# Order of selections, logits, one-hot transposes and scatters in a mixture-of-experts stage

## The reference

```python
grouped = x.reshape(B, S // t, t, D)                 # t = 16 tokens in a group
cont_logits = jnp.einsum('bgtd,des->bgtes', grouped, controller) + tie
cont_perm = (cont_logits == jnp.max(cont_logits, axis=-3, keepdims=True))
intermediate = jnp.einsum('bgtd,desf->bgtesf', grouped, f1)
inner = jax.nn.relu(jnp.einsum('bgtesf,bgtes->bgesf', intermediate, cont_perm))
inter2 = jnp.einsum('bgesf,esfd->bgesd', inner, f2)
result = jnp.einsum('bgesd,bgtes->bgtd', inter2, cont_perm)
```

## Time and profile before

| | us |
|---|---|
| median of 3 runs (lowest, highest) | 752.02 (750.18, 753.73) |
| the profiled execution's own time | 753.89 |
| its span, first to last instruction | 752.0 |
| PE busy | 711.2 (95%) |
| DVE busy | 595.7 (79%) |
| ACT busy | 544.2 (72%) |
| chain that ended last, share of PE | 86% |
| chain that ended last, share of DVE and of DMA | 6% and 2% |

### The profile page before, as it was taken

How to read it: one execution, slowest core, us unless ns; L and a number is a source line. 1 busy time by engine, 2 the same in 40 slices (tenths; PEclk the granted TensorE clock), 3 DMA queues, 4 the chain that set the end, 5 groups by cost and what they waited for, 6 DMA issues and landing times.

```text
span 752.0 us, 22953 instructions
## 1 busy us (share of the span) xinstructions
PE 711.2 (95%) x7420; PEld 575.8 (77%) x7420; DVE 595.7 (79%) x2418; ACT 544.2 (72%) x1606; POOL 181.2 (24%) x375
## 2 busy tenths in 40 slices
PE   8899999999999999999999999989879979878888
PEld 7788888888888888888888888866656656655666
DVE  6698898898988988989889888986656756656566
ACT  4788989898889898988899889874445344344243
POOL 2130321302303213023032130646705506400000
PEclk9999999999999999999999999998999999999999
DMA  6776787677867877778678767746099798798943
GB/s 179 185 184 143 185 196 163 166 187 166 193 147 177 194 164 167 185 168 193 150 174 194 166 144 157 158 87 218 3 394 300 261 388 276 265 383 271 342 164 104
DMA packets 110742, 149.24 MB, mean 198 GB/s; under 512 B 14784, under 2 KB 75712, under 8 KB 110432
## 3 DMA queue, kind: packets, MB, share of 16 engines
q1 hardware_dynamic: 107904, 146.26, 72.0%
q10 hardware_dynamic: 2592, 1.71, 1.0%
q0 software_dynamic: 192, 0.52, 0.2%
HBM read 39.39 MB, written 33.55 MB: 97 GB/s over the span
## 4 chain that ended last, share of the span: by engine, by line
PE 86%; DVE 6%; issue 3%; DMA 2%; ACT 2%; SPq 1%; POOL 0%; DVEq 0%; POOLq 0%
PE bank L672 15%; PE bank L624 15%; PE bank L659 8%; PE bank L685 8%; PE bank L696 8%; PE bank L646 7%; PE bank L819 5%; PE bank L861 3%; DVE stage L1503 3%; PE bank L904 3%; DMA stage<-scratch 2%; PE bank L717 2%; PE bank L877 2%; PE bank L617 2%; PE bank L704 2%
## 5 line engine op out<-in xcount | busy, mean ns | idle before, releaser
L1026 ACT ACTIVATE Ps<-Ps,nmax 128x256 f32<-128x256 f32 x512 | 254.6, 501 | 19.8 <-DVE nmax L1246 19.8
L1246 DVE CUSTOM_DVE_ANT_0 Ps<-bank,masks 128x256 f32<-128x256 f32 x512 | 193.0, 421 | 28.6 <-issue 28.4
L672 PE MATMUL bank<-ident,Ps 128*128 128x128 f32 x1024 | 134.8, 274 | 2.5 <-ACT Ps L1026 1.8
L672 PEld LDWEIGHTS bank<-ident,Ps 128*128 128x128 f32 x1024 | 114.8, 141 | 11.9 <-issue 3.3
L624 PE MATMUL bank<-hT,WT 128*128 128x256 f32 x512 | 121.1, 380 | 0.3 <-ACT hT L983 0.3
L624 PEld LDWEIGHTS bank<-hT,WT 128*128 128x128 f32 x512 | 92.4, 190 | 10.7 <-ACT Vs L999 0.7
L549 POOL TENSOR_SCALAR h<-X,mv,roots 128x256 f32<-128x256 f32 x64 | 79.6, 1255 | 78.7 <-PE bank L819 76.5
L1026 ACT ACTIVATION_READ_ACCUMULATOR Ps<-Ps,nmax 128x1 f32 x512 | 97.4, 190 | 0.0
L659 PE MATMUL bank<-stack 128*128 128x256 f32 x512 | 91.5, 311 | 0.6 <-DMA stack<-parts 0.6
L1257 DVE COPY PTs<-bank 128x512 f32<-128x512 f32 x128 | 86.7, 677 | 0.2
L659 PEld LDWEIGHTS bank<-stack 128*128 128x128 f32 x512 | 71.7, 189 | 17.3 <-issue 13.1
(11 more groups left out here) (107 smaller groups left out, 1052.9 us busy)
## 6 DMA issues: line engine op xcount, KB each, us to landing
stack<-parts SPq DMA_DIRECT2D x506, 128.0 KB, 2.5
scratch<-stage SPq DMA_DIRECT2D x48, 512.0 KB, 4.3
stage<-scratch SPq DMA_DIRECT2D x96, 256.0 KB, 4.4
X<-in_x SPq DMA_DIRECT2D x32, 256.0 KB, 2.9
out<-X SPq DMA_DIRECT2D x32, 256.0 KB, 3.7
rbc<-turned SPq DMA_DIRECT2D x126, 64.0 KB, 2.1
f1s<-in_L_ffn_f SPq DMA_DIRECT2D x1, 2048.0 KB, 8.5
f2s<-in_L_ffn_f SPq DMA_DIRECT2D x1, 2048.0 KB, 14.2
```

The lines of the kernel that those rows point to most:

```text
L672: last = nc.tensor.transpose(PTb[h % 2][:, k * N + t * P:k * N + t * P + P], Ps[:, pr % 2, t, h % 2, k * P:k * P + P], ident[:, :])
L1026: last = nc.scalar.activation(Ps[:, pr % 2, t, h, :], Ps[:, pr % 2, t, h, :], ACT.Exp, bias=nmax[:, pr % 2, t, h:h + 1], scale=-1.0, accum ...
L1246: last = nc.vector.tensor_tensor_reduce(out=Ps[:, pr % 2, t, h, :], in0=s_bank(n)[:, h * N:h * N + N], in1=masks[:, t, :], scale=1.0, scal ...
```

## The change

It does four things.

1. In each unit the one-hot transpose leaves its place between the first and second selection and goes between the third and fourth, with bank 3 in place of bank 2. It then waits until DVE has finished the pair that was in bank 3 (`fin_done`; in unit 1 of chunk 0 `res_done`). Unit 0 of chunk 0 keeps its place. ACT's save of it moves in the same way.
2. The logits no longer wait for the saved one-hot (`perm_saved`), but for DVE's comparison (`perm_done`).
3. A unit's first scatter moves from behind the third selection to behind the first; its second stays behind the fourth and waits in addition for `perm_saved`. On DVE the maximum now stands in front of the third save, and the first `finish` between the first and second save.
4. In the last chunk the units scatter pairs 0 and 1, then 2, then 3 and 4, and the expert stage pairs 5, 6, 7 in rounds 1, 2, 3; its three-way rotation of banks starts two rounds later, at round 4.

```diff
+        def scatters(c, u):
+            return ((), (0, 1), (2, 3), (4, 5))[u] if c < CHUNKS - 1 else ((), (0, 1), (2,), (3, 4))[u]
+        def late(c, w):
+            return {0: 6, 1: 7}.get(w) if c < CHUNKS - 1 else {1: 5, 2: 6, 3: 7}.get(w)
+        TWO_PAIRS = 4
...
             def logits(n, into=bank[2]):
-                if n > 0:
+                if n > AHEAD:
+                    pe.wait_ge(perm_done, n)
+                elif n > 0:
                     pe.wait_ge(perm_saved, n)
...
                 select(n, 0)
-                if n + 1 < CHUNKS * UNITS:
-                    one_hot_transpose(n + 1)
                 if n == 0:
+                    one_hot_transpose(1)
                     o_project(B - 1, True)
+                if pairs:
+                    scatter(c - 1, pairs[0])
                 select(n, 1)
                 if ahead:
                     logits(n + AHEAD)
                 select(n, 2)
-                if pairs:
-                    scatter(c - 1, pairs[0])
+                if 0 < n < CHUNKS * UNITS - 1:
+                    if c > 0:
+                        pe.wait_ge(fin_done, (c - 1) * (CT // 2) + (pairs[0] + 1 if pairs else 0))
+                    elif n == 1:
+                        pe.wait_ge(res_done, B)
+                    one_hot_transpose(n + 1, bank[3])
                 select(n, 3)
-                if pairs:
+                if len(pairs) > 1:
+                    pe.wait_ge(perm_saved, min(n + 2, CHUNKS * UNITS))
                     scatter(c - 1, pairs[1])
...
             def unit(c, u):      # DVE
                 save_selected(c, u, 0)
                 late_root_steps(c, u, 0)
+                if pairs:
+                    finish(c - 1, pairs[0])
                 save_selected(c, u, 1)
...
                     tied_logits(n + AHEAD)
-                save_selected(c, u, 2)
                 late_root_steps(c, u, 2)
                 if ahead:
                     group_maximum()
-                if pairs:
-                    finish(c - 1, pairs[0])
+                save_selected(c, u, 2)
                 save_selected(c, u, 3)
```

More of the change, by code:

```diff
@@ L337, in second_bank @@
         def second_bank(c, w, hf):
-            if c < CHUNKS - 1 or w < len(LATE):
+            if c < CHUNKS - 1 or w < TWO_PAIRS:
                 return 4 + 2 * hf
-            return (2, 4, 6)[(2 * (w - len(LATE)) + hf) % 3]
+            return (2, 4, 6)[(2 * (w - TWO_PAIRS) + hf) % 3]
         def products(c, q, hf):
@@ L839, in contract @@
                 pe.wait_ge(in_dve, n + 1)
-                if c == CHUNKS - 1 and w == len(LATE):
+                if c == CHUNKS - 1 and w == TWO_PAIRS:
                     pe.wait_ge(fin_done, c * (CT // 2))
                     pe.wait_ge(st_act, 2 * n)
-                elif c == CHUNKS - 1 and w > len(LATE):
+                elif c == CHUNKS - 1 and w > TWO_PAIRS:
                     pe.wait_ge(st_act, 2 * n)
@@ L912, in unit @@
                 ahead = n + AHEAD < CHUNKS * UNITS
-                pairs = scatters(u) if c > 0 else ()
+                pairs = scatters(c, u) if c > 0 else ()
                 if ahead:
@@ L941, in experts @@
                         expand(c, w + 1)
-                    if c > 0 and w < len(LATE):
-                        scatter(c - 1, LATE[w])
+                    if c > 0 and late(c, w) is not None:
+                        pe.wait_ge(perm_saved, min((c + 1) * UNITS + 1, CHUNKS * UNITS))
+                        scatter(c - 1, late(c, w))
                     contract(c, w)
@@ L1104, in unit @@
                 save_selected(c, u, 0)
-                if n + 1 < CHUNKS * UNITS:
-                    save_one_hot(n + 1)
+                if n == 0:
+                    save_one_hot(1)
                 save_selected(c, u, 1)
                 save_selected(c, u, 2)
+                if 0 < n < CHUNKS * UNITS - 1:
+                    save_one_hot(n + 1, bank[3])
                 save_selected(c, u, 3)
@@ L1493, in experts @@
                 for w in range(TWOS):
-                    if c > 0 and w < len(LATE):
-                        finish(c - 1, LATE[w])
+                    if c > 0 and late(c, w) is not None:
+                        finish(c - 1, late(c, w))
                     dve.wait_ge(f2_ready, c * TWOS + w + 1)
```

3 lines of the change are left out of this document (removed).

## The result

The changed kernel takes 757.07 us in the median of 20 runs (753.14 to 761.71), against 752.92 for the kernel before in 20 runs beside it. The ratio is 1.0059, with an interval of 1.004 to 1.0077: slower by 0.6%, a little more than the 0.5% that can be told from no change. The profiled execution took 759.59 with a span of 757.7; before it was 753.89 and 752.0. Its mean clock was 0.981, before 0.988.

A forecast was written before the change was run, and what follows sets the result against it. PE, 86% of the chain, was taken as the bound. Chunk 0 +1.0 - 1.5, chunk 1 +0.9, chunk 2 +0.6, chunk 3 -2.6 and clock +5.1 gave +3.5 on the median 752.02: 755.5 us, range 750 to 760.

The forecast's parts named there:

- The first pair comes before its data: Unit 1 of chunks 1 to 3: PE reaches the first pair before its gathers land, waiting 1.9, 1.8 and 1.6 us.
- The clock: Behind the new first-pair waits in chunks 1 to 3: PE falls to the low clock, 1.7 us each, +5.1 in all.
- the expand at 538.97: Chunk 0: the low clock there, with 64 records in 3.25 against 1.93, would stay away, -1.5 us.
- The rival that the clock holds: Chunks 1 to 3: waits come but no low clock follows, -1.6 us, 750.4; chance 0.20.
- The long low clock: Rival behind the first-pair waits: low clock goes on, 3.4 us per place, 760.6 if at all three; chance 0.20.
- the gathers are no obstacle: Rival: first half-1 gathers land 2 us sooner or PE comes later, about -5.1 us, 747; chance 0.10.
- The steady unit: Units 2 and 3 of chunks 1 and 2: 7.65 us, -0.24 each, with DVE's third save late next.
- The wait for `perm_saved` and bank 3: Steady unit: the new `perm_saved` wait is over before the pair; bank 3 late only in the +0.2 bound.
- Chunk 0: Units without scatters 6.65 against 6.49 us, fourth selection of unit 0 about 0.7 later; +1.0 - 1.5 in sum.
- The wait for tile 15: Expert stage: the scatter's wait for tile 15's gather goes, -0.8 us in chunk 1 and -1.6 in chunk 2.
- Chunk 3: Last chunk: unit 1 ends 1.8 late, rounds 1 to 3 are 3.1 apart, round 4 at 712.5 against 715.12: -2.6 us.
- Chunks 1 and 2: Sums of late unit 1, shorter later units and missing tile 15 wait: +0.9 and +0.6 us before the clock.

The follow-up runs named there:

- experiment 1: Changed kernel, but unit 1 of chunks 1 to 3 keeps the order of before on PE, ACT and DVE: 750.03 us, ratio to before 0.9938.
- experiment 2: Kernel before with only the new places of the last chunk's scatters (part 4): 748.52 us, ratio 0.9947.
- experiment 3: Changed kernel with sixteen unused matrix products ahead of the first pair in unit 1 of chunks 1 to 3: 755.95 us, ratio 1.0029.
- experiment 7: Changed kernel with nine unused matrix products ahead of the first pair in unit 1 of chunks 1 to 3: 754.02 us, ratio 1.0013.
- experiment 5: Changed kernel with PE's new order only in units 2 and 3 of chunks 1 to 3, third save in its old place everywhere: 745.3 us, ratio 0.9901.
- experiment 4: Changed kernel with DVE's third save back between tie breaker and maximum: 753.69 us, ratio 1.001.
- Experiment 8: Changed kernel without its fourth part, so the new order in all units with the last chunk's old scatter places: 759.51 us, ratio 1.0088.
- experiment 6: Kernel before with part 4 and six unused products ahead of the fourth selection in chunk 0's first unit: 750.72 us, ratio 0.9985.

## Why the prediction was right, and where it was off

The forecast was 755.5 in 750 to 760; measured was 757.07, +4.15 to the kernel before where I had +3.5. By its own terms:

**The first pair comes before its data: confirmed.** It was the term that decides, and experiment 1 puts its whole cost at 7 us or more. Its three sizes (1.9, 1.8, 1.6) came out as 2.79, 1.13 and 2.62: two too small and one too large. I had carried over the time to landing from before. The gathers in question took longer here. By line, half 1 of tiles 0 and 1 in chunks 1, 2 and 3 of the changed kernel, against 4.2, 4.0 and 3.7 for tile 0 in before:

```profile
L450 SPq DMA_DIRECT2D stage<-scratch x2: 580/598/617, 567.1 to 567.7; - x2
DMA to landing us min/median/max: 5.0/5.0/5.0
...
L450 SPq DMA_DIRECT2D stage<-scratch x2: 580/598/616, 623.9 to 624.5; - x2
DMA to landing us min/median/max: 4.6/4.6/4.6
...
L450 SPq DMA_DIRECT2D stage<-scratch x2: 580/598/616, 679.5 to 680.1; - x2
DMA to landing us min/median/max: 4.4/4.4/4.5
```

In chunk 1 this is 0.8 us more to landing, and the issue, at 567.1 - 560.55 = 6.5 behind the chunk's start, is 0.25 later than before's 6.3: 1.8 (572.5 - 570.7, which I had put down as 1.9) + 0.8 + 0.25 = 2.85, measured 2.79. In chunk 3 it is 0.7 and 0.4: 1.6 + 0.7 + 0.4 = 2.7, measured 2.62. In chunk 2 the issue was 5.4 behind the start instead of 6.4: the low clock had stretched the last contract of the stage before from 1.08 to 2.02 us and so put off the start, and the issue came 7.4 to 7.5 behind that contract's start in both kernels. With 0.6 more to landing that makes 1.8 - 1.0 + 0.6 = 1.4, and PE came 0.2 later to the pair; the wait was 1.13. The layout was right; only the landing time is no constant.

**The clock: right in kind, its size too small.** I had 5.1 for three places, less 1.5 for the expand at 538.97. That expand did take 1.95 in the changed kernel, but the -1.5 was a wrong reading: it took as long in every profile but before's, experiment 2's with the old order among them, so nothing shows that the order had made the clock low there. In the changed kernel's profile the low clock followed two of the three new waits (2.79 and 2.62, not 1.13), and it came at 616, 698 and 728 as well, where I had nothing. Over all runs the loss is 11.4 against 4.3 to 5.0: +6.8 where I had +3.6. The rival that the clock holds is out: its condition, no more loss than before, is not met in the mean of 20 runs. Experiments 1, 3 and 7 show that the new waits cause half of it or more; where the rest comes from is open.

The Trainium skill ("TensorE: Matmul & The Clock Gate", section "Why this matters for your kernels") has the clock fall mid-kernel behind idle gaps longer than any of these. None here was as long, and the clock fell behind 2.79 and 2.62, to 0.57 and 0.59 over the next four microseconds: the measurement decides, and it forbids reading the rule the other way round, namely that shorter waits are free.

**The long low clock: not in this kernel's chunks 1 to 3**, where each stretch cost about what I had taken (4.0 x (1 - 0.57) = 1.7 in 572:576). It exists, though: in experiment 5's chunk 3 a wait of 1.68 for a gather at 680.57 was followed by

```profile
681.00:692.00 11.00, 10.14 (x112) 7.35 (x108) 4.48 (x7) 3.31 (x6) 0.00 (x0) 0.53 0.61 199
```

and it was the fastest kernel all the same. That the gathers are no obstacle is refuted by every profile with the new order in unit 1.

**The steady unit: right.** 7.67 against 7.65, by the late third save, which experiment 4 confirms: 7.53 without it. The wait for `perm_saved` and bank 3 cost nothing, as worked out. **Chunk 0: right** in its units (6.69 against 6.65); the wait of its fourth selection grew from 1.47 to 2.13, by 0.66 where I had 0.7. Its sum was not: +0.35 from the first unit's start to chunk 1 in the two profiles, where +1.0 - 1.5 = -0.5 was forecast. **The wait for tile 15: right.** It is gone in chunks 1 and 2: round 1's contract comes 5.81 and 5.82 behind the stage's start, before 6.66 and 7.47, so -0.85 and -1.65 for the predicted 0.8 and 1.6.

**Chunk 3: the term that was mis-sized.** I had worked out -2.6 for it, plus 1.7 for the clock, so -0.9 up to round 4; its profile shows +2.4. The rounds themselves fit (3.0 apart for 3.1), and part 4 alone gives -2.3. The 3.3 us between are, for the most part, the first wait (2.6 instead of 1.6: 1.0), the second low clock at 698 (at most 1.7), which I had not foreseen behind waits of 0.57 and 0.86 for DVE's saves in a stage without logits and transposes, and 0.4 of idle inside round 1's scatter, for which the profile shows no wait. I had taken the low clock that before has at 690 to go with the wait of 0.90 ahead of it; but in the profiles of experiments 1, 2 and 4 unit 3's first scatter also takes 1.94 where 1.07 is the time at full clock. Chunks 1 and 2 were off as well, in opposite directions: with 1.7 of clock each they had +2.6 and +2.3, and the profile shows +4.0 and -0.6. All this is one execution: over all runs the work and waits of the whole change came out 2 us better than before, where my terms without the clock make -0.1, and the clock 3.2 worse. Experiment 8 has the order's work and waits at +0.1, where my terms for chunks 0 to 2 make +2.5, and experiment 2 has those of part 4 at -2.9 for my -2.6. The two errors nearly cancel in +4.15: the direction and the deciding wait were worked out, but that the time came so close to 755.5 is luck.

## What to carry to other kernels

When an instruction is moved earlier in an engine's queue, compare its new time with the landing of its data before counting what its old place cost: here that one comparison, in one unit of four, decided the sign. A pair that is consumed early also frees its buffer early and keeps the queue of transfers short, so the same move can be wrong in the unit that follows a write and right in the ones behind it; try it by units, not all at once. And price a wait on PE twice, once for its length and once for the clock behind it.

## What the hardware showed that I had not expected

- Useless work can be better than waiting: nine unused products ahead of the first pair brought 757.07 down to 754.02, and sixteen, which with 3.84 us outlast the wait of 2.79, cost no more than the bare wait (755.95), with the lost time down from 11.4 to 5.0 us.
- The clock doesn't follow the idle time alone. In chunk 0 an idle of 2.13 us was followed by a clock of 0.50 in 514:524 of the changed kernel, and in experiment 3, which has the same code there, the same idle of 2.13 by a clock of 1.00:

```profile
514.00:524.00 10.00, 9.80 (x75) 7.38 (x76) 4.70 (x13) 3.14 (x6) 4.89 (x4) 0.50 0.36 111
```

```profile
514.00:524.00 10.00, 8.60 (x116) 6.63 (x116) 7.29 (x18) 5.47 (x11) 7.22 (x6) 1.00 0.38 120
```

  The first is the changed kernel, the second experiment 3: 75 records against 116 in the same ten microseconds. Of the five profiles with this idle of 2.13, two (experiments 3 and 7) kept the clock at 1.00 and three did not. What decides between them isn't seen in these profiles. Single runs of one kernel spread by it: in experiment 6 the run with the mean clock of 0.998 took 746.28 and one with 0.986 took 755.27.
- The first gather of a half 1 took 3.7 to 5.0 us from issue to landing in the three chunks of the two kernels, at places that the code treats alike, so a wait behind one has to be given as a range of a microsecond.
